# Local attention projections as three float32r products of split rows and weights

## What is computed

```python
def _ln(x, w, b):
    m = x.mean(-1, keepdims=True)
    v = ((x - m) ** 2).mean(-1, keepdims=True)
    return (x - m) * jax.lax.rsqrt(v + 1e-05) * w + b

def local_attn(x, Wqkv, Wout):          # W = 64, H = 8, DH = 64
    qkv = x @ Wqkv.T                    # x is _ln(x, ln_w, ln_b); 512 x 128 by 128 x 1536 per batch
    q, k, v = jnp.split(qkv, 3, axis=-1)
    ...
    ke, ve = (expand(k), expand(v))     # each window of 64 sees itself and both neighbours
    sim = jnp.einsum('bhnid,bhnjd->bhnij', q, ke) * SCALE
    sim = jnp.where(valid[None, None, :, None, :], sim, -1000000000.0)
    attn = jax.nn.softmax(sim, axis=-1)
    o = jnp.einsum('bhnij,bhnjd->bhnid', attn, ve)
    o = o.transpose(0, 2, 3, 1, 4).reshape(b, n, H * DH)
    return o @ Wout.T
```

## Time and profile before

| | |
|---|---|
| runs | 1962.52, 1966.30, 1966.01 us; median 1966.01 |
| profiled execution | 1961.81 us, span 1959.6 us |
| TensorE busy | 1800.0 us, 92% |
| VectorE busy | 1494.3 us, 76% |
| ScalarE busy | 1461.5 us, 75% |
| GpSimd busy | 616.4 us, 31% |
| mean granted TensorE clock | 0.976 of full speed |
| local attention, first block | about 456 to 1004 us of the span |
| local attention, second block | about 1272 to 1785 us of the span |

### The profile page before, as it was taken

The page is one execution under the profiler, slowest core; times in us unless marked ns, Lnnn a source line. Parts: engine busy times, 40 slices in busy tenths (PEclk is TensorE's granted clock), DMA queues, the critical chain, the costliest instruction groups (busy, mean ns, idle before and its releaser), DMA issues. The chain is left out here.

```text
span 1959.6 us, 67406 instructions
## 1 busy us (share of the span) xinstructions
PE 1800.0 (92%) x27305; PEld 1282.9 (65%) x27305; DVE 1494.3 (76%) x3598; ACT 1461.5 (75%) x4168; POOL 616.4 (31%) x732
## 2 busy tenths in 40 slices
PE   4898898988999999999979988899999999997998
PEld 2444444444677777777768865567777777776786
DVE  8999999996676777777876766657776767788674
ACT  4999999984788888887735547678888888774554
POOL 1000000001344444444453317334444444344431
PEclk7999999998999999999989999999999999999999
DMA  6555655530001010101020000010101010102111
GB/s 196 146 134 148 159 142 144 140 81 12 13 14 24 13 24 14 24 14 24 15 55 2 1 1 1 2 24 13 24 13 24 14 24 14 24 13 50 30 33 33
DMA packets 77917, 91.88 MB, mean 47 GB/s; under 512 B 11485, under 2 KB 67650, under 8 KB 77090
## 3 DMA queue, kind: packets, MB, share of 16 engines
q1 hardware_dynamic: 76314, 87.15, 17.8%
q10 hardware_dynamic: 1296, 0.44, 0.1%
HBM read 39.67 MB, written 31.10 MB: 36 GB/s over the span
## 5 line engine op out<-in xcount | busy, mean ns | idle before, releaser
L1420 POOL TENSOR_TENSOR f1l_pn<-f1l_p,f1l_rs 128x512 f32<-128x512 f32 (+1 forms) x256 | 207.5, 832 | 324.4 <-DVE f1l_rs L1141 323.6
L1420 POOL TENSOR_TENSOR f2l_pn<-f2l_p,f2l_rs 128x512 f32<-128x512 f32 (+1 forms) x256 | 207.5, 832 | 297.8 <-DVE f2l_rs L1141 297.7
L1022 ACT ACTIVATE f2l_p<-f2l_sm,f2l_nb 128x192 f32<-128x192 f32 x512 | 211.5, 433 | 44.4 <-DVE f2l_nb L1134 44.4
L1022 ACT ACTIVATE f1l_p<-f1l_sm,f1l_nb 128x192 f32<-128x192 f32 x512 | 211.3, 432 | 42.4 <-DVE f1l_nb L1134 42.4
L514 ACT ACTIVATE r_pr<-r_far 128x1536 f32<-128x1536 f32 x128 | 195.6, 1528 | 4.3 <-PE r_far L388 4.0
L404 PE MATMUL r_acc<-r_pr,r_vp 128*32 128x128 f32 (+2 forms) x3584 | 193.8, 333 | 5.1 <-DVE r_pr L617 3.9
L609 DVE SCALAR_TENSOR_TENSOR r_pr<-r_pr,k_lo,r_cap 128x512 f32<-128x512 f32 x256 | 179.5, 742 | 8.5 <-ACT r_pr L514 8.3
L617 DVE TENSOR_SCALAR r_pr<-r_pr,k_hi,k_lo 128x768 f32<-128x768 f32 x256 | 161.6, 672 | 0.0
L514 ACT ACTIVATE r_pr<-r_near 128x1024 f32<-128x1024 f32 x128 | 139.9, 1093 | 1.1 <-PE r_near L375 1.1
L818 PE MATMUL f1l_pj<-f1l_xt,k_wqkv 128*128 128x512 f32 x244 | 132.6, 625 | 2.6 <-ACT f1l_kt L1004 1.4
L1425 POOL MEMSET k_rtz<- 128x608 f32 x1 | 0.6, 604 | 426.7 <-POOLq L668 426.7
(11 more groups left out here) (450 smaller groups left out, 4994.0 us busy)
## 6 DMA issues: line engine op xcount, KB each, us to landing
rbf_rows<-r_part SPq DMA_DIRECT2D x112, 128.0 KB, 2.2
r_qs<-rbf_rows SPq DMA_DIRECT2D x60, 192.0 KB
r_ks<-rbf_rows SPq DMA_DIRECT2D x60, 192.0 KB
f1l_vs<-f1l_vv SPq DMA_DIRECT2D x64, 128.0 KB, 2.4
f2l_vs<-f2l_vv SPq DMA_DIRECT2D x64, 128.0 KB, 2.4
rbf_rows<-r_part SPq DMA_DIRECT2D x16, 384.0 KB, 2.7
rbf_rows<-r_part SPq DMA_DIRECT2D x16, 256.0 KB, 3.1
out<-k_x SPq DMA_DIRECT2D x16, 256.0 KB, 2.3
```

The costliest lines, as they stand in the source:

```text
L1022: ins = nc.scalar.activation(p[:, u % 2, k, :], sm[:, u % 2, k // 2, k % 2 * PW:(k % 2 + 1) * PW], ACT.Exp, bias=nb[:, u % 2, k:k + 1], ac ...
L1420: ins = nc.gpsimd.tensor_tensor(pn[:, u % 2, at:at + HU * w].rearrange("p (k c) -> p k c", k=HU), p[:, u % 2, :, cols], r.broadcast_to([P, ...
```

## The change

The projections' single float32 matmul becomes three float32r matmuls into the same bank: with rows x = xh + xl and weights w = wh + wl, each part float32r, it adds wl xh, wh xh and wh xl (wl xl is left out). For q and k the order is wl xh, wh xh, wh xl, for v it is xl wh, xh wl, xh wh.

- The rows: TensorE transposes them in the same place as before (`turn_x`, in i = 3 for the batch after the next), ScalarE writes `xt` as before (`leave_x`). Then GpSimd casts `xt` to `xh` and subtracts to get `xl` (`split`), behind both `normalise` of that step. `xh` and `xl` have two buffers each. The first projection of a batch waits for `xh` (semaphore `s_xs`), and its third product for `xl`. For batch 0 VectorE does the splitting (`split_first`); for batch 1 GpSimd, after the first two `normalise`.
- The weights: `wqkv` leaves the list of later loads. Its thirds are loaded by SyncE behind batches 1, 2 and 3 of the RBF stage to a tile `whole`, and GpSimd, idle there, casts and subtracts each to `wqkv_h` and `wqkv_l`.
- Room for these in SBUF: `yt` becomes a part of `qt`, `one` a single column that is broadcast, and the small tiles of the RBF stage are freed at its end.
- Counting: the transposed rows have semaphores of their own (`s_xp`, `s_xe`), and `USES` goes from 13 to 12.

The diff, cut to its core:

```diff
@@ stage_rbf
             for b in range(B):
                 batch(b, b % 2)
+                if 0 <= b - SPLIT_AT < 3:
+                    q = b - SPLIT_AT
+                    wait(sp, s_wh, 2 * q)
+                    sp.dma_start(whole[:], A["wqkv"][:, THIRD * q:THIRD * (q + 1)]).then_inc(s_wl, 16)
...
+            for q in range(3):
+                w = slice(THIRD * q, THIRD * (q + 1))
+                pool.wait_ge(s_wl, 16 * (q + 1))
+                nc.gpsimd.tensor_copy(K["wqkv_h"][:, w], whole[:]).then_inc(s_wh, 1)
+                pool.wait_ge(s_wh, 2 * q + 1)
+                nc.gpsimd.tensor_tensor(K["wqkv_l"][:, w], whole[:], K["wqkv_h"][:, w], ALU.subtract).then_inc(s_wh, 1)
@@ stage_light
+        xh = sb("xh", [P, 2, S], F32R)
+        xl = sb("xl", [P, 2, S], F32R)
...
-            yt = sb("yt", [P, 2, S])
+            yt = qt[:, 1, 0:2, :]
...
-        USES = 1 + 2 * HP + NT
+        USES = 2 * HP + NT
+        TURN_AT = NT - 1
...
-        one = sb("one", [R2, S])
+        one = sb("one", [R2, 1])
@@ TensorE, use(b, k)
+                if k == 1:
+                    pe.wait_ge(s_xs, 2 * b + 1)
+                if k <= 2 * HP:
                     c = (k - 1) // 2 + (k - 1) % 2 * HP
-                    mm = nc.tensor.matmul(at, K["wqkv"][:, c * P:(c + 1) * P], xt[:], start=True, stop=True)
+                    w = slice(c * P, (c + 1) * P)
+                    nc.tensor.matmul(at, w_l[:, w], xh[:, par, :], start=True, stop=False)
+                    nc.tensor.matmul(at, w_h[:, w], xh[:, par, :], start=False, stop=False)
+                    if k == 1:
+                        pe.wait_ge(s_xs, 2 * b + 2)
+                    mm = nc.tensor.matmul(at, w_h[:, w], xl[:, par, :], start=False, stop=True)
                 else:
                     j = k - 1 - 2 * HP
-                    mm = nc.tensor.matmul(at, xt[:, j * P:(j + 1) * P], K["wqkv"][:, 2 * H * DH:3 * H * DH],
-                                          start=True, stop=True)
+                    rows, w = slice(j * P, (j + 1) * P), slice(2 * H * DH, 3 * H * DH)
+                    nc.tensor.matmul(at, xl[:, par, rows], w_h[:, w], start=True, stop=False)
+                    nc.tensor.matmul(at, xh[:, par, rows], w_l[:, w], start=False, stop=False)
+                    mm = nc.tensor.matmul(at, xh[:, par, rows], w_h[:, w], start=False, stop=True)
...
+            def turn_x(b):
+                if b == 1:
+                    pe.wait_ge(s_pe, 2 * HP + (0 if C else 1))
+                elif b > 1:
+                    pe.wait_ge(s_pt, UNITS * (b - 2) + 2 * TURN_AT + 2)
+                pe.wait_ge(s_z, b + 1)
+                at = bank(b, 0)
+                for j in range(NT):
+                    mm = nc.tensor.transpose(at[:, j * P:(j + 1) * P], z[:, j, :], K["ident"][:])
+                mm.then_inc(s_xp, 1)
@@ VectorE
+            def split_first():
+                dve.wait_ge(s_xe, 1)
+                nc.vector.tensor_copy(xh[:, 0, :], xt[:]).then_inc(s_xs, 1)
+                dve.wait_ge(s_xs, 1)
+                nc.vector.tensor_tensor(xl[:, 0, :], xt[:], xh[:, 0, :], ALU.subtract).then_inc(s_xs, 1)
@@ GpSimd
+            def split(b):
+                par = b % 2
+                pool.wait_ge(s_xe, b + 1)
+                wait(pool, s_pp, USES * (b - 1))
+                nc.gpsimd.tensor_copy(xh[:, par, :], xt[:]).then_inc(s_xs, 1)
+                pool.wait_ge(s_xs, 2 * b + 1)
+                nc.gpsimd.tensor_tensor(xl[:, par, :], xt[:], xh[:, par, :], ALU.subtract).then_inc(s_xs, 1)
...
             for t in range(T):
                 if t + 1 < T:
                     normalise(2 * t + 2)
                     normalise(2 * t + 3)
+                if t % NT == TURN_AT and t // NT + 2 < B:
+                    split(t // NT + 2)
                 if t % NT == 1 and t // NT + 2 < B:
                     scaled(t // NT + 2)
```

More of the change, by code:

```diff
@@ L178, in stage_rbf @@
         s_late = sem("late")
+        s_wl = sem("wl")
+        s_wh = sem("wh")
         s_ini = sem("ini")
@@ L911, in output @@
                     mm.then_inc(s_w, 1)
-            for k in range(1 + 2 * HP):
+            turn_x(0)
+            for k in range(1, 1 + 2 * HP):
                 use(0, k)
@@ L943, in _ @@
                         scores(3)
-                use(1, 0)
+                turn_x(1)
             else:
-                for k in range(1 + 2 * HP, USES):
+                for k in range(1 + 2 * HP, USES + 1):
                     use(0, k)
-                use(1, 0)
+                turn_x(1)
                 scores(2)
@@ L1008, in leave, with leave_x @@
                 ins.then_inc(s_pe, 1)
+            def leave_x(b):
+                act.wait_ge(s_xp, b + 1)
+                wait(act, s_xs, 2 * b)
+                nc.scalar.activation(xt[:], bank(b, 0), ACT.Identity, scale=K["ln_w"][:, 0:1],
+                                     bias=K["ln_b"][:, 0:1]).then_inc(s_xe, 1)
             def leave_late(n):
@@ L1063, in _ @@
             nc.scalar.preload_act_table_set("natural_log_exp_and_others")
-            for k in range(1 + 2 * HP):
+            leave_x(0)
+            for k in range(1, 1 + 2 * HP):
                 leave(0, k)
@@ L1328, in _ @@
                 link(nc.vector.reciprocal(K["r2"][:], two[:, 0, :]))
-                for b in range(1, 9):
+                rows(1)
+                split_first()
+                for b in range(2, 9):
                     rows(b)
@@ L1385, in step @@
                     reciprocals(2 * t + 2)
-                late = t % NT == NT - 1 and t // NT + 2 < B
+                late = t % NT == TURN_AT and t // NT + 2 < B
                 if t and not late:
@@ L1439, in _ @@
             normalise(1)
+            split(1)
             for t in range(T):
@@ L2171, in program @@
         K["rtz"] = sb("rtz", [P, 2 * B * (B - 1) + P])
-        for n in ("lo", "hi"):
-            K[n] = sb(n, [P, RH])
-        stage_rbf(nc, K, A)
+        for n in ("wqkv_h", "wqkv_l"):
+            K[n] = sb(n, [P, 3 * H * DH], F32R)
+        K["later"], loads = loads, []
+        load("ident", A["c_ident"], [P, P])
+        with ExitStack() as early:
+            own = lambda n, s, d=F32: early.enter_context(nc.sbuf_tensor("k_" + n, s, d))
+            for n in ("norm_sel", "later_key"):
+                load(n, A["c_" + n], [P, A["c_" + n].shape[1]], own)
+            for n in ("wq", "wk", "wv", "wo"):
+                load(n, A[n], [P, E], own)
+            load("gam", A["gam"].partition_broadcast(P), [P, RH], own)
+            load("gam_p", A["gam_p"], [P, 1], own)
+            for n in ("lo", "hi"):
+                K[n] = own(n, [P, RH])
+            K["first"] = loads
+            stage_rbf(nc, K, A)
         C = {n: sb("c_" + n, [P, 1]) for n in ("dt", "mag", "th", "n", "sin", "cos", "t", "lr", "li", "den",
```

66 lines of the change are left out of this document (28 added, 38 removed).

## The result

The changed kernel takes 1944.96 us (median of 4 runs, 1944.7 to 1945.16) where the kernel before took 1964.26 on the same chip (4 runs, 1962.31 to 1966.3): a ratio of 0.9902, 95% interval [0.9884, 0.9919]. That is faster by 19.3 us; 31 were forecast. The profiled execution took 1944.7 us, its span is 1942.9 against 1959.6, so 16.7 us are to be explained between the two traces.

What follows compares the result with a forecast made beforehand. Bound: a mixed loop of maxima, exponentials, first copy-out, TensorE from the second projection to `values`, `late` and sum. Two stages' 29.4 us plus 1 us net per prologue made 31 off the 1966.0 median: 1935 us, range 1911 to 1954.

Steps and rivals of the forecast that it cites:

- The bound of a projection: Local attention steps: with one bank, the second projection waits for ScalarE's copy-out of the first, 3.11 us after the maxima start.
- rival (a): Local attention: TensorE's work alone is the loop, the copy-outs having slack; 53 us off, 1913 us; chance 0.16.
- The wait for `xl`: Step i = 0: the first projection's third product waits some 0.8 us for GpSimd's subtraction; second projection 0.41 us later.
- a product is 0.22: Projections: each 512-wide float32r product takes 0.22 us, so a projection takes 0.66 us and saves 0.20 us.
- 15 x: Each local attention stage: 15 batches gain 0.40 + 0.40 + 0.19 us each, less 14 edges of 0.01: 14.7 us.
- 0.9 net to the first GpSimd split: Prologue of each stage: about 0.9 us lost to the first GpSimd split, which directly follows the copy to `xt`.
- The list of what would make the prediction wrong: Signs: i = 1 at 7.25, i = 0 above 8.5, products at 0.24 or more, or a lower granted clock in new gaps.
- At nothing I cost the splitting of the weights: RBF stage: three loads and 1.95 us of GpSimd each cost nothing, GpSimd being idle there; without that cover 6 us.
- rival (d): Batch edges: `xl` comes late, say by waits for SBUF beside VectorE; 1.4 us later gives 1974 us; chance 0.10.
- (b): Local attention: TensorE alone is the loop and the split is hidden too; 1890 us; chance 0.03.
- (e): Projections: float32r at 512 columns takes as many passes as float32; 660 us slower; chance 0.01.
- (c): Local attention: loops through ScalarE and VectorE hold more than counted, or a product costs 0.24; half the gain, 1950 us; 0.14.

Runs made afterwards that it cites:

- less in the first: Against the changed kernel, from batch 1 on the first projection of steps i = 1, 2 and 3 has two products instead of three; 1948.2 us (one run).
- second trace: The changed kernel profiled once more, with no edit, beside the kernel before on one chip; median 1945.71 us, ratio 0.9918.

## Why the prediction was right and wrong

**Right.** The bound of a projection: the second projection at M+3.11 in i = 1, behind the copy-out, is there to the hundredth, and a product less in the first projection moves nothing. That TensorE's gain turns into waits, so that 72 us of saved work come out as some 20, was the main choice against rival (a), and it holds. The wait for `xl` was forecast to end with the third product at M+2.20 and measured at M+2.08; the second projection at M+3.62 and measured at M+3.44. The wait was to be some 0.8 us: the third product could have started 0.23 us behind the second and started 0.51 later than that. The step i = 0 came out even (7.71 against 7.73).

**The median batch came out almost as forecast, by luck: two errors cancel.** 0.98 us less were forecast and 0.94 and 0.92 measured (medians of the second and of the first block). But the term "a product is 0.22" was wrong. It is 0.23, nearer to twice the 256-wide row than to the quarter of a float32 matmul, and the pause stays in each group: 0.80 against 0.96 saves 0.16 for the second projection, 0.08 in the pause ahead of the third, and 0.09 in the third, together 0.33 in i = 1 and 2 where 0.40 were forecast. In i = 3 it was 0.28 for 0.19.

**"15 x" was the step that cost most.** The forecast gave the median step's gain to all of them. 48 steps of each block (the third to the fiftieth interval) gave 9.6 and 9.4 us where 12 batches of 0.98 are 11.8; the ten behind them gave 0.4 and 2.5. Together 7.3 us of the missing 14. The median batch itself is a small part of it. Most is in long steps, which the sum did not have: all steps from the third to the sixtieth interval of both blocks together stand 12.8 us over the second block's medians before and 19.0 in the changed kernel. TensorE's pauses without a named releaser went from 2.9 to 8.9 us in the same intervals. The largest is in the first block's fifty-first interval, which grew from 9.37 to 10.29: it holds a pause of 1.19 us, and in the trace of "less in the first", which has none there, it is 9.14. So a pause can lengthen its step by about its own length; that they make up most of the rest is argued from their sizes and places, and their own cause stays open. Beside them, VectorE's picking of the routed rows takes a smaller part: there steps i = 1 and 2 take 7.62 and 7.69 us, a gain of 0.23 and 0.17 where the median step gained 0.32.

**The opening steps were one of the terms mis-sized**: "0.9 net to the first GpSimd split" is 1.9 and 2.5 (0.8 and 2.5 in the second trace). I had counted the split's time but not that it is queued behind `normalise(1)`, so that TensorE has nothing to do for 2.2 us, nor a lower granted clock behind it. The list of what would make the prediction wrong had the clock, but no price. Without the wait (15.63 and 8.14 us) the clock stays up as well.

**"At nothing I cost the splitting of the weights" failed**: 2.1 us between the two traces. The size is loose: in the ten traces with this RBF stage its last sum starts from 448.94 to 453.13, 451.0 in the median, and of before there is one trace, with 448.88. I named the idle GpSimd as cover and did not ask what VectorE, busy for 415 of 430 us there, shares with it. The Trainium skill (GPSIMD Engine Reference, Specifications) does say that GpSimd shares its SBUF interfaces with VectorE, in contention with VectorE's instructions of two SBUF inputs; the pair of such instructions that went from 1.40 to 2.42 us agrees. For the light stage I had named that danger, as rival (d), and there it did not come: 0.61 and 1.28 us.

**The rivals.** (a) and (b) are excluded by the first-projection run, (d) by `xl` at M+2.03, (e) by 0.23 us a product. (c) was given half the gain: the time is its 1950 less 5, and part of its mechanism is real.

## What to carry to other kernels

When a step is a ring of engines, price an edit by the stretch between the last foreign wait and the next one, and then look for the second ring: here three stood within 0.1 us. Taking one product out of each place in turn finds them in three runs. Look separately at a stage's first steps and at steps with extra work; a median step times the count overstates a gain. And where an idle engine takes over work, ask first what the full engine beside it shares with it, then move the work to where its result is wanted one whole step later: here one constant gave 10 us.

## What the runs showed of the hardware

- Float32r matmuls 128x512 into one bank follow each other at 0.23 us at the 2.4 GHz level and 0.43 at 1.2 GHz; the first of a group after other work has 0.30 to 0.34.
- GpSimd's cast and subtraction (0.61 and 1.26 us alone) and VectorE's two-operand instruction on SBUF (0.70) stretch each other when they overlap: 1.08, 1.64, and 2.42 for a pair. At the batch edges of the local attention the same GpSimd operations kept their time.
- In the second block's opening the granted clock fell to the 1.2 GHz level in all ten traces in which TensorE had stood idle for about 0.45, 1.65 and 0.56 us in turn, and not in the one in which it stood idle for 0.44 and 1.65 us alone. In the first block waits of 1.63 and 0.56 us brought it down in seven traces of nine.
- TensorE pauses in which the profile names no releaser, 0.2 to 1.2 us each and most of them inside a run of small matmuls, came in the same 13 steps in two traces of one kernel: 8.9 and 10.5 us in all, against 2.9 in the kernel before.
